# Mixture-of-experts kernel: order of gathers, scatters and row turns around experts 1 to 4

## The chip, the cores and the metric

One core of a Trainium2 chip runs the whole program. The metric is the device time of one execution in microseconds (us). Engine names follow the profile: PE is TensorE, DVE is VectorE, ACT is ScalarE, POOL is GpSimd, SP issues plain DMAs.

## The reference, cut to what matters

```
for e in range(64):                       # first layer, 4096 tokens, top 8 of 64 experts
    inp = xin[e]                          # the 256 rows (tokens) routed to e, 1024 wide
    h   = silu(inp @ wg[e]) * (inp @ wu[e])          # 1024 -> 384, twice
    out = h @ wd[e]                                  # 384 -> 1024
    y[tok] += out * w[tok, e]                        # w: routing weight of the row
x = x + y
# then a second layer: x @ W.T plus adapters, plus a gated low-rank part
```

The rows are first conditioned by a per-sample 128x128 matrix, and a softmax over 64 logits with a top-8 choice decides which rows an expert gets. All of it is float32; the change touches only the expert loop.

## The kernel before, in words

**Stages.** Up to about 173 us the kernel conditions the rows, writes them to the scratch tensor `yd`, and builds the routing tables. Then 64 experts follow, numbered 0 to 63, until about 1789 us. Then comes the second layer.

**One expert on PE.** `up(e)` is three blocks (numbered n = 3e to 3e+2, 128 of the 384 hidden columns each), each with a g half and a u half; `down(e)` follows and takes the hidden rows of one block after another (j = 0, 1, 2). float32 products are made of high and low float32r parts: `HR` and `LR` for weights, the halves of `XX` for the rows, `hH` and `hL` for the hidden values. Two pairs of PSUM banks take the blocks in turn, so block n may start only when `join(n-2)` has emptied its banks. `down(e)` may start on a bank only when `result(e-1)` has read it, and its step j needs `low_h(3e+j)`.

**Weights.** Six units of 768 KB for each expert (`gA uA gB uB dA dB` from expert 2 on). SP loads unit n into one of four `raw` slots once DVE's `split` of unit n-4 is done. `split` on ACT (L1235) writes the high part, `split` on DVE (L1770) the low part.

**Rows.** POOL gathers the rows of expert e in eight indirect DMAs, `gather_x(e, 0)` and `gather_x(e, 1)` with four each (L662), into `Xg`. `turn_x(e, c)` on DVE (L1788) transposes one half into `XR`, `high_x` on ACT (L1263) and `low_x` on DVE (L1794) split it into `XX`. `gather_x(e+1, c)` may be issued only after `turn_x(e, c)`. The row numbers come from `gather_tab(e)` (L637), `count`, `token`, `spread` and `index`.

**Results.** `copy_2(n)` on ACT (L1271) and `join(n)` on DVE (L1806) read the banks of a block; `silu`, `product` (L1812), `high_h`, `low_h` (L1816) make the hidden values. `gather_w(e)` (L672) fetches the routing weights into one of two buffers `Wg`; `column(e)` on DVE (L1837) takes the one column of it that is needed; `result(e, c, h)` on ACT (L1289) scales the output of `down(e)` with it into `ot`, four times for each expert. `scatter(e)` (L684, two DMAs of 512 KB) adds `ot` to the accumulator in HBM. `result(e)` waits for the completion of `scatter(e-1)`, since `ot` is one buffer, and for `column(e)`.

**Order.** Every engine's order is written out by hand. For experts 0 to 2 the lists stand in full; from expert 3 on DVE and ACT run a loop, and POOL's loop starts at `scatter(1)`. Each waits on semaphores, in order: whatever is queued behind a waiting instruction of an engine waits too.

POOL's order before, from the gathers of expert 2 on: x(2), w(1), tab(4), scatter(0), x(3), w(2), w(3), tab(5), scatter(1), x(4), w(4), tab(6), scatter(2), x(5), w(5), and so on.

Of the kernel before, what the change touches and what calls it, by code (L numbers as in the profile page):

```python
# [16 lines left out]
E = 64  # L17
# [42 lines left out]
def adaln_ffn_kernel(nc, x, cond, adap, w0, gate_w, wg, wu, wd, W, A, Bm, scal,  # L60
# [14 lines left out]
    with ExitStack() as ctx:  # L75
# [526 lines left out]
        def _(eng):  # L602
# [63 lines left out]
            def gather_w(e):  # L666
                if e >= 2:
                    eng.wait_ge(s_wc, e - 1)
                else:
                    eng.wait_ge(d_wy, 16 * NB // 4)  # L670
                for c in range(2):
                    eng.indirect_dma_start(Wg[:, e % 2, c, :], None, wdr,  # L672
                                           bass.IndirectOffsetOnAxis(ap=toki[:, c * E + e:c * E + e + 1], axis=0))\
                       .then_inc(d_wg[e % 2], 16)
# [17 lines left out]
            gather_w(0)  # L692
            gather_x(2, 0)
            gather_x(2, 1)
            gather_w(1)
            gather_tab(4)
            scatter(0)
            gather_x(3, 0)
            gather_x(3, 1)
            gather_w(2)  # L700
            gather_w(3)
            for e in range(2, E + 1):
                if e < E - 3:
                    gather_tab(e + 3)
                scatter(e - 1)
                if e + 2 < E:
                    gather_x(e + 2, 0)
                    gather_x(e + 2, 1)
                    gather_w(e + 2)
            eng.wait_ge(d_sc, 32 * E)  # L710

            def gather_a(t):
# [423 lines left out]
        def _(eng):  # L1136
# [223 lines left out]
            for e in range(2, E):  # L1360
                if e < E - 2:
                    spread(e + 2)
                if e == 2:
                    copy_2(6)
                    result(1, 0, 0)
                    silu(6)
                    result(1, 0, 1)
                    result(1, 1, 0)
                    high_h(6)
                    result(1, 1, 1)  # L1370
                    high_x(3, 0)
                    split("dB", 2)
                    high_x(3, 1)
                else:
                    for o in range(4):
                        result(e - 1, o // 2, o % 2)
                    if e < E - 1:
                        high_x(e + 1, 0)
                        high_x(e + 1, 1)
                    if e < E - 1:  # L1380
                        split("dB", e)
                    else:
                        split("dA", e)
                    copy_2(3 * e)
                    if e == E - 1:
                        split("dB", e)
                    silu(3 * e)
                    high_h(3 * e)
                if e + 1 < E:
                    split("gA", e + 1)  # L1390
                copy_2(3 * e + 1)
                silu(3 * e + 1)
                high_h(3 * e + 1)
                if e + 1 < E:
                    split("uA", e + 1)
                else:
                    eng.wait_ge(s_dn, 4 * (E - 1))
                    eng.wait_ge(d_la, 16 * 64)
                    high_w(0)
                copy_2(3 * e + 2)  # L1400
                silu(3 * e + 2)
                high_h(3 * e + 2)
                if e + 1 < E:
                    for k in ("gB", "uB", "dA")[:3 if e + 1 < E - 1 else 2]:
                        split(k, e + 1)
# [167 lines left out]
        def _(eng):  # L1573
# [229 lines left out]
            def join(n):  # L1803
                b0 = 2 * (n % 2)
                eng.wait_ge(s_c2, n + 1)
                eng.tensor_tensor(gu[:, :, :], ps[:, b0:b0 + 2, 0:CAP], gu[:, :, :], ALU.add).then_inc(s_gs, 1)  # L1806
# [71 lines left out]
            product(3)  # L1878
            low_h(3)
            index(3)  # L1880
            split("dB", 1)
            join(4)
            split("gA", 2)
            product(4)
            turn_x(2, 0)
            low_h(4)
            turn_x(2, 1)
            join(5)
            low_x(2, 0)
            product(5)  # L1890
            low_x(2, 1)
            low_h(5)
            column(1)
            for k in ("uA", "gB", "uB"):
                split(k, 2)
            count(4)
            token(4)
            split("dA", 2)
            join(6)
            turn_x(3, 0)  # L1900
            product(6)
            low_h(6)
            turn_x(3, 1)
            index(4)
            low_x(3, 0)
            split("dB", 2)
            join(7)
            count(5)
            product(7)
            token(5)  # L1910
            low_h(7)
            low_x(3, 1)
            column(2)
            column(3)
            split("gA", 3)
            join(8)
            product(8)
# [20 lines left out]
            for e in range(3, E):  # L1938
                if e < E - 1:
                    turn_x(e + 1, 0)  # L1940
                    turn_x(e + 1, 1)
                    if e + 2 < E:
                        index(e + 2)
                    low_x(e + 1, 0)
                    low_x(e + 1, 1)
# [5 lines left out]
                    turn_b(3)  # L1951
                    split("dA", e)
                join(3 * e)
                if e < E - 1:
                    column(e + 1)
                product(3 * e)
                low_h(3 * e)
                split("dB", e)
# [326 lines left out]
```

## Time and profile before

| | |
|---|---|
| median of 3 runs | 2349.42 us (2349.35 to 2352.59) |
| the profiled execution, its own time | 2363.11 us |
| its span, first to last instruction | 2361.4 us |
| busy: PE, DVE, ACT, POOL | 98%, 76%, 60%, 57% |
| PE clock, mean over the span | 0.996 of full speed |

Read it so: the profiled execution is 13.7 us longer than the median run, so differences are taken inside the trace and carried over to the median. PE is busy nearly all the time, so what counts is where PE is idle or at half clock. The timelines give for each instruction its start, its duration and, in brackets, how long its engine had been idle and what ended that.

### The profile page before, as it was taken

Reading aid. Unit: us, or ns where it says so; the run is one execution under the profiler, and the core shown is the slowest. Engines: PE = TensorE matmul, PEld = TensorE weight load, DVE = VectorE, ACT = ScalarE, POOL = GpSimd, SP = SyncE. Lnnn points to the kernel's source line nnn. Section 1 sums busy time; section 2 is a strip of 40 time slices with the busy share of each in tenths; the row PEclk is TensorE's granted clock in tenths of the full one; section 3 lists DMA queues with packets and bytes.
Section 4 is the critical chain, followed back from the end, with each engine's and each line's share of the span. In section 5 each row is a group of like instructions: output and inputs, shape, how many; then the busy total and the mean of one; then the engine's idle time right before and its main releaser. Section 6 shows DMA issues by size and latency. Waiting matters only on the chain.

```text
span 2361.4 us, 35519 instructions
## 1 busy us (share of the span) xinstructions
PE 2319.7 (98%) x12530; PEld 2036.3 (86%) x12530; DVE 1788.6 (76%) x3091; ACT 1419.2 (60%) x2341; POOL 1340.8 (57%) x999
## 2 busy tenths in 40 slices
PE   6989899999999999999999999999999999999999
PEld 4768788888888888888888888888888999999999
DVE  4888788888888888888788888888874268666665
ACT  4766677777777777777777777777763122222221
POOL 4117887777777777877778777777740011111110
PEclk8999999999999999999999999999999999999999
DMA  8999898989999999989989899899895544544452
GB/s 291 379 311 337 260 283 277 283 286 283 279 284 296 271 286 288 278 278 285 284 275 283 283 282 284 272 290 281 274 273 132 112 113 127 146 132 131 132 140 83
DMA packets 256339, 582.35 MB, mean 247 GB/s; under 512 B 85665, under 2 KB 113698, under 8 KB 256162
## 3 DMA queue, kind: packets, MB, share of 16 engines
q1 hardware_dynamic: 189186, 401.19, 52.2%
q0 software_dynamic: 55584, 160.02, 26.3%
q10 hardware_dynamic: 11392, 18.88, 2.1%
q8 instruction: 99, 1.62, 0.3%
q14 instruction: 78, 0.64, 0.1%
HBM read 456.25 MB, written 123.45 MB: 245 GB/s over the span
## 4 chain that ended last, share of the span: by engine, by line
PE 91%; DVE 3%; DMA 2%; issue 2%; ACT 1%; SPq 0%; another core or an unknown queue 0%; ACTq 0%; POOL 0%; DVEq 0%; POOLq 0%
PE ps L891 25%; PE ps L904 21%; PE ps L890 12%; PE ps L1006 9%; PE ps L999 7%; PE ps L951 4%; PE ps L887 4%; PE ps L760 2%; PE ps L989 2%; PE ps L888 2%; PE ps L770 1%; DMA raw<-in_L_ffn_wd 1%; PE ps L963 1%; DVE LR L1770 1%; DMA bx<-in_L_ffn_base_w 1%
## 5 line engine op out<-in xcount | busy, mean ns | idle before, releaser
L891 PE MATMUL ps<-XX,HR 128*128 128x512 f32 x2688 | 959.7, 396 | 0.0
L890 PE MATMUL ps<-XX,LR 128*128 128x256 f32 x2688 | 750.3, 279 | 0.6 <-DVE LR L1770 0.5
L662 POOL DMA_INDIRECT Xg<-yd,idx x504 | 653.4, 1296 | 160.0 <-issue 153.0
L1770 DVE TENSOR_TENSOR LR<-raw,HR 128x1536 fp32r<-128x1536 f32 x384 | 657.5, 1752 | 5.6 <-ACT HR L1235 4.7
L891 PEld LDWEIGHTS ps<-XX,HR 128*128 128x128 f32 x2688 | 505.0, 188 | 104.2
L1235 ACT ACTIVATE HR<-raw 128x1536 fp32r<-128x1536 f32 x384 | 556.9, 1479 | 18.0 <-DMA raw<-in_L_ffn_wd 11.9
L890 PEld LDWEIGHTS ps<-XX,LR 128*128 128x128 f32 x2688 | 507.3, 189 | 18.9 <-DVE LR L1770 1.2
L684 POOL DMA_INDIRECT accd<-ot,toki x128 | 254.0, 1984 | 160.4 <-ACT ot L1289 139.7
L904 PE MATMUL ps<-LR,hH 128*128 128x512 f32 x768 | 302.5, 394 | 0.0
L904 PE MATMUL ps<-HR,hH 128*128 128x512 f32 x768 | 298.6, 389 | 3.0 <-DVE hL L1816 3.0
L904 PE MATMUL ps<-HR,hL 128*128 128x512 f32 x768 | 301.0, 392 | 0.0
L1806 DVE TENSOR_TENSOR gu<-ps,gu 128x512 f32<-128x512 f32 x192 | 132.7, 691 | 161.4 <-ACT gu L1271 146.2
L723 POOL DMA_INDIRECT m8a<-m8d,midx x32 | 36.9, 1153 | 337.3 <-PE ps L963 333.1
L1271 ACT ACTIVATE gu<-ps 128x512 f32<-128x512 f32 x192 | 113.5, 591 | 148.0 <-issue 82.6
L637 POOL DMA_INDIRECT G<-tabd,rowi x124 | 168.8, 1361 | 40.4 <-issue 37.2
L672 POOL DMA_INDIRECT Wg<-wdr,toki x128 | 158.1, 1235 | 39.0 <-issue 38.7
L904 PEld LDWEIGHTS ps<-HR,hH 128*128 128x128 f32 x768 | 144.2, 188 | 33.9 <-DVE hL L1816 4.3
L904 PEld LDWEIGHTS ps<-HR,hL 128*128 128x128 f32 x768 | 144.2, 188 | 33.4
L999 PE MATMUL ps<-MH,xT 128*128 128x392 f32 x640 | 172.7, 341 | 0.0
L1275 ACT ACTIVATE sil<-gu 128x256 f32<-128x256 f32 x192 | 80.2, 418 | 149.6 <-DVE gu L1806 145.6
L904 PEld LDWEIGHTS ps<-LR,hH 128*128 128x128 f32 x768 | 144.4, 188 | 28.8
L887 PE MATMUL ps<-XX,HR 128*128 128x512 f32 x384 | 152.4, 397 | 5.9 <-DVE gu L1806 3.9
(262 smaller groups left out, 3868.8 us busy)
## 6 DMA issues: line engine op xcount, KB each, us to landing
raw<-in_L_ffn_wd SPq DMA_DIRECT2D x128, 768.0 KB
raw<-in_L_ffn_wg SPq DMA_DIRECT2D x126, 768.0 KB
raw<-in_L_ffn_wu SPq DMA_DIRECT2D x126, 768.0 KB
yd<-yrow ACTq DMA_DIRECT2D x32, 512.0 KB
x<-accd SPq DMA_DIRECT2D x32, 512.0 KB, 3.9
out<-x SPq DMA_DIRECT2D x31, 512.0 KB, 5.6
xt<-in_x SPq DMA_DIRECT2D x25, 512.0 KB
accd<-xt SPq DMA_DIRECT2D x25, 512.0 KB
```

The lines of the kernel that those rows point to most:

```text
L637: eng.indirect_dma_start(G[:, e % 2, c, :], None, tab, bass.IndirectOffsetOnAxis(ap=rowi[:, c * E + e:c * E + e + 1], axis=0))\
L662: eng.indirect_dma_start(Xg[:, c, q, :], None, yd4, bass.IndirectOffsetOnAxis(ap=idx4[:, e % 4, i:i + 1], axis=0))\
L672: eng.indirect_dma_start(Wg[:, e % 2, c, :], None, wdr, bass.IndirectOffsetOnAxis(ap=toki[:, c * E + e:c * E + e + 1], axis=0))\
L684: eng.indirect_dma_start(acc, bass.IndirectOffsetOnAxis(ap=toki[:, c * E + e:c * E + e + 1], axis=0), ot[:, c, :], None, compute_op=ALU.ad ...
L887: eng.matmul(bank(out), wh, xx, start=True, stop=False)
L890: eng.matmul(bank(out, 0, CAP), wl, xx[:, 0:CAP], start=False, stop=False)
L891: mm = eng.matmul(bank(out), wh, xx, start=False, stop=(k == 7))
L904: mm = eng.matmul(bank(4 + o), X[:, j, c * P:(c + 1) * P], Wt[:, s, j * 512:(j + 1) * 512], start=(j == 0 and m == 0), stop=(j == 2 and m ...
L999: mm = eng.matmul(bank(BK[region], 0, HG), X[:, k, :], (MH, ML, MH)[m][:, k, a:a + HG], start=(i == 0), stop=(i == 23))
L1006: mm = eng.matmul(bank(BK[region], 0, HG), (XH, XH, XL)[m][:, k, :], (YH, YL, YH)[m][:, k, :], start=(first and i == 0), stop=(i == 11), s ...
L1235: eng.activation(HR[:, (n + 2) % NHL, :], raw[:, n % NRAW, :], ACT.Copy).then_inc(s_H, 1)
L1770: eng.tensor_tensor(LR[:, (n + 2) % NHL, :], raw[:, n % NRAW, :], HR[:, (n + 2) % NHL, :].bitcast(F32), ALU.subtract).then_inc(s_L, 1)
```

## The change

Three things are reordered; no arithmetic is changed.

1. POOL: `gather_tab(4)` and `gather_x(3)` are issued before `scatter(0)`; `gather_tab(5)` and `gather_x(4)` before `scatter(1)`. `gather_w(1)` moves behind `scatter(0)`, `gather_w(2)` and `gather_w(3)` behind `scatter(1)`; from expert 3 on the loop issues `gather_w(e+1)` where it issued `gather_w(e+2)`.
2. DVE: `turn_x(2, 0)`, `turn_x(2, 1)` and `turn_x(3, 0)` go to earlier places, `split("gA", 2)` goes behind `low_h(4)`, `low_x(3, 1)` behind `join(7)`. `column(1)`, `column(2)` and `column(3)` go to later places, and in the loop `column(e)` stands where `column(e+1)` stood.
3. ACT: in iteration 2 the four `result(1)` go from around `copy_2(6)` and `silu(6)` to behind `split("dB", 2)`, and `high_x(3, 1)` goes ahead of that split.

```diff
@@ -692,21 +692,26 @@
             gather_w(0)
             gather_x(2, 0)
             gather_x(2, 1)
-            gather_w(1)
             gather_tab(4)
-            scatter(0)
             gather_x(3, 0)
             gather_x(3, 1)
+            scatter(0)
+            gather_w(1)
+            gather_tab(5)
+            gather_x(4, 0)
+            gather_x(4, 1)
+            scatter(1)
             gather_w(2)
             gather_w(3)
-            for e in range(2, E + 1):
+            for e in range(3, E + 1):
                 if e < E - 3:
                     gather_tab(e + 3)
                 scatter(e - 1)
                 if e + 2 < E:
                     gather_x(e + 2, 0)
                     gather_x(e + 2, 1)
-                    gather_w(e + 2)
+                if e + 1 < E:
+                    gather_w(e + 1)
             eng.wait_ge(d_sc, 32 * E)
 
             def gather_a(t):
@@ -1362,15 +1367,13 @@
                     spread(e + 2)
                 if e == 2:
                     copy_2(6)
-                    result(1, 0, 0)
+                    high_x(3, 0)
                     silu(6)
-                    result(1, 0, 1)
-                    result(1, 1, 0)
                     high_h(6)
-                    result(1, 1, 1)
-                    high_x(3, 0)
+                    high_x(3, 1)
                     split("dB", 2)
-                    high_x(3, 1)
+                    for o in range(4):
+                        result(1, o // 2, o % 2)
                 else:
                     for o in range(4):
                         result(e - 1, o // 2, o % 2)
@@ -1878,40 +1881,39 @@
             product(3)
             low_h(3)
             index(3)
+            turn_x(2, 0)
             split("dB", 1)
             join(4)
+            turn_x(2, 1)
+            product(4)
+            low_h(4)
             split("gA", 2)
-            product(4)
-            turn_x(2, 0)
-            low_h(4)
-            turn_x(2, 1)
             join(5)
             low_x(2, 0)
             product(5)
             low_x(2, 1)
             low_h(5)
-            column(1)
-            for k in ("uA", "gB", "uB"):
-                split(k, 2)
+            split("uA", 2)
+            turn_x(3, 0)
+            split("gB", 2)
+            split("uB", 2)
             count(4)
             token(4)
             split("dA", 2)
             join(6)
-            turn_x(3, 0)
+            turn_x(3, 1)
             product(6)
+            index(4)
             low_h(6)
-            turn_x(3, 1)
-            index(4)
             low_x(3, 0)
+            column(1)
             split("dB", 2)
             join(7)
+            low_x(3, 1)
+            product(7)
             count(5)
-            product(7)
+            low_h(7)
             token(5)
-            low_h(7)
-            low_x(3, 1)
-            column(2)
-            column(3)
             split("gA", 3)
             join(8)
             product(8)
@@ -1938,6 +1940,8 @@
             for e in range(3, E):
                 if e < E - 1:
                     turn_x(e + 1, 0)
+                    if e == 3:
+                        column(2)
                     turn_x(e + 1, 1)
                     if e + 2 < E:
                         index(e + 2)
@@ -1951,8 +1955,7 @@
                     turn_b(3)
                     split("dA", e)
                 join(3 * e)
-                if e < E - 1:
-                    column(e + 1)
+                column(e)
                 product(3 * e)
                 low_h(3 * e)
                 split("dB", e)
```

## Rows read from the trace of the kernel before

**Rows 1.** The page: span, and its part 1 (busy time by engine).
```profile
span 2361.4 us, 35519 instructions
...
PE 2319.7 (98%) x12530; PEld 2036.3 (86%) x12530; DVE 1788.6 (76%) x3091; ACT 1419.2 (60%) x2341; POOL 1340.8 (57%) x999
```

**Rows 2.** By stretch: from:to, length, busy by engine, PEclk, DMA share, GB/s.
```profile
226.41:243.20 16.79, 16.79 (x97) 14.67 (x96) 11.91 (x19) 11.53 (x20) 13.44 (x12) 1.00 0.74 270
243.20:253.89 10.69, 8.42 (x37) 6.61 (x37) 9.57 (x19) 6.30 (x8) 8.86 (x7) 1.00 0.96 231
253.89:276.68 22.79, 18.89 (x99) 16.10 (x98) 15.96 (x24) 14.00 (x23) 18.83 (x14) 0.93 0.94 291
269.26:276.68 7.42, 7.42 (x33) 6.39 (x34) 6.47 (x15) 4.89 (x7) 6.20 (x5) 0.77 1.01 246
...
301.70:1750.00 1448.30, 1448.30 (x7642) 1237.50 (x7641) 1184.87 (x1608) 1060.10 (x1617) 1124.20 (x803) 1.00 0.92 282
```

**Rows 3.** Timeline of PE: start, us, line, operation, [idle before <-releaser].
```profile
251.14 0.50 PE L904 MATMUL ps<-HR,hH 128*128 128x512 f32 x1 [2.27 <-DVE hL L1816]
...
254.01 0.40 PE L887 MATMUL ps<-XX,HR 128*128 128x512 f32 x1
...
269.26 0.51 PE L887 MATMUL ps<-XX,HR 128*128 128x512 f32 x1 [3.90 <-DVE gu L1806]
```

**Rows 4.** Timeline of DVE, experts 1 to 3.
```profile
212.37 1.76 DVE L1770 TENSOR_TENSOR LR<-raw,HR 128x1536 fp32r<-128x1536 f32 x1 [0.81 <-issue]
...
223.41 5.10 DVE L1770 TENSOR_TENSOR LR<-raw,HR 128x1536 fp32r<-128x1536 f32 x3 [0.26 <-ACT HR L1235]
...
238.82 1.25 DVE L1788 STREAM_TRANSPOSE XR<-Xg 128x1024 f32<-128x1024 f32 x1 [2.78 <-DMA Xg<-yd,idx]
...
248.58 0.69 DVE L1806 TENSOR_TENSOR gu<-ps,gu 128x512 f32<-128x512 f32 x1
...
258.64 1.76 DVE L1770 TENSOR_TENSOR LR<-raw,HR 128x1536 fp32r<-128x1536 f32 x1 [2.55 <-ACT HR L1235]
...
264.29 1.25 DVE L1788 STREAM_TRANSPOSE XR<-Xg 128x1024 f32<-128x1024 f32 x1 [2.73 <-DMA Xg<-yd,idx]
```

**Rows 5.** Timeline of ACT, experts 2 and 3.
```profile
240.10 1.07 ACT L1263 ACTIVATE XX<-XR 128x1024 fp32r<-128x1024 f32 x1 [1.61 <-issue]
...
242.45 0.57 ACT L1271 ACTIVATE gu<-ps 128x512 f32<-128x512 f32 x1
...
257.12 1.49 ACT L1235 ACTIVATE HR<-raw 128x1536 fp32r<-128x1536 f32 x1 [3.72 <-DMA raw<-in_L_ffn_wd]
...
260.11 2.42 ACT L1289 ACTIVATE ot<-ps,wcol 128x512 f32<-128x512 f32 x4
...
265.57 1.06 ACT L1263 ACTIVATE XX<-XR 128x1024 fp32r<-128x1024 f32 x1 [2.09 <-issue]
...
267.90 0.58 ACT L1271 ACTIVATE gu<-ps 128x512 f32<-128x512 f32 x1
```

**Rows 6.** Timeline of POOL: gathers and scatters issued.
```profile
212.55 2.40 POOL L637 DMA_INDIRECT G<-tabd,rowi  x1 [0.30 <-issue]
...
232.62 0.95 POOL L662 DMA_INDIRECT Xg<-yd,idx  x1 [0.30 <-issue]
...
244.76 1.58 POOL L684 DMA_INDIRECT accd<-ot,toki  x1 [0.30 <-issue]
...
258.48 0.95 POOL L662 DMA_INDIRECT Xg<-yd,idx  x1 [0.30 <-issue]
```

**Rows 7.** Timeline of SP's queue: weight loads issued.
```profile
248.70 4.46 SPq L435 DMA_DIRECT2D raw<-in_L_ffn_wd  x2
```

**Rows 8.** DMA traffic by stretch (last two columns), as in rows 2.
```profile
241.00:242.00 1.00, 1.00 (x8) 0.86 (x7) 1.00 (x2) 1.00 (x2) 1.00 (x1) 1.00 0.00 0
...
248.00:252.00 4.00, 1.73 (x8) 1.11 (x7) 3.04 (x5) 2.20 (x4) 3.33 (x3) 1.00 1.04 202
...
253.00:260.00 7.00, 7.00 (x41) 6.02 (x40) 4.45 (x3) 3.12 (x9) 5.47 (x6) 1.00 1.05 396
```

## The prediction

> **What bounds the kernel now.** I read the page first, then the busy time by stretch, then PE's timeline, and then went back through DVE, ACT, POOL and the DMA traffic to what was late. PE is busy 98% of the span [rows 1]. By stretch, it has no idle time at all from 301.70 to 1750 us [rows 2], so nothing that is moved in the loop can gain there; it can only lose. Around the change the picture is different. One expert takes PE 25.02 us: 16.79 for its three blocks [rows 2] and 8.23 for its down part (25.02 less 16.79). From the start of up(2) at 226.41 to the start of down(3) at 276.68 there are two ups and one down, 41.8 us of work, in 50.27 us [rows 2]: 8.5 us are lost. They lie in three places:
> - 2.27 us before step j = 2 of down(2), which waits for low_h(8) [rows 3] and makes the 8.23 into 10.69 [rows 2];
> - 3.90 us before block n = 11, the last of up(3), which waits for join(9) [rows 3];
> - 1.83 us in that block, which takes 7.42 us in place of a third of 16.79, at a mean granted clock of 0.77: after the idle 3.90 us the clock stood at its lower level, 1.2 GHz, for a time [rows 2].
>
> The rest, about 0.5 us, is small gaps. Both waits go back to rows that arrive late. DVE waited 2.78 us for the second half of expert 3's rows and 2.73 us for that of expert 4 [rows 4]; ACT's high_x stood idle behind them for 1.61 and 2.09 us [rows 5]. A third thing is late before block 11: ACT waited 3.72 us for the weight unit dA(3) [rows 5], and DVE 2.55 us behind it [rows 4]. So 8.5 us, 0.36% of the run, is the most that the change can remove.
>
> **Rows gathered earlier.** How long a gather takes to issue follows from DVE: the issue at 212.55 began inside the split of 212.37 to 214.13 [rows 4] and ended at 214.95 [rows 6], 0.8 after it, where one outside a split takes 0.95 and a gap of 0.30 [rows 6]. From 212.55 to 244.76 POOL issued 19 DMAs one behind another [rows 6], 1.7 us each on average, gaps included. After the change gather_x(3, 0) can start when turn_x(2, 0), now at 211.6, is through, at 212.9. Eight issues at 1.7 end at 226.3. In the trace a last gather landed 5.25 us after its issue ended (233.57 to 238.82) and another 4.86 us after (259.43 to 264.29) [rows 4, 6]; so expert 3's rows are there by 231.5 at the latest, and turn_x(3, 1), due after join(6) at 233.9, does not wait. That removes the 2.78. turn_x(4, 1) loses its 2.73 in the same way: its gathers end near 249.3 in place of 259.43.
>
> **What takes the place of it in iteration 2.** turn_x(3, 0), 1.25 us [rows 4], now stands between the splits of uA(2) and gB(2). The three splits took 5.10 from 223.41, 1.70 each [rows 4], so gB(2) ends at 223.4 + 1.7 + 1.2 + 1.7 = 228.0 or 228.1. PE wants it half way through its first g half, a quarter of a 5.6 us block: 226.41 + 1.4 = 227.8. That is a new stall of 0.3 to 0.4 us; I take 0.4. The bounds are 0 (the split 0.3 earlier) and 1.0 (turn_x(3, 0) waits for its rows). The same insertion delays token(4) and spread(4), which follow the splits: these end at 228.5 + 1.2 = 229.7, count(4), token(4) and spread(4) take some 2.9 more, and copy_2(6) starts at about 232.6. From there ACT has, in order, 0.5 + 1.0 + 0.4 (copy, high_x, silu), 1.0 of waiting for product(6), 0.4 + 1.0 + 1.4 (high_h, high_x, split dB), 2.4 for the four results and 1.4 for split gA(3), the durations by [rows 5]: 9.5 us, and copy_2(7) starts at 242.1. Before it started at 242.45 [rows 5]. **This is the point of the forecast: the wait is gone, but the four results, 2.4 us, now stand in the gap.** Before, low_h(8) was ready for PE 8.7 us after copy_2(7) began (251.14 less 242.45) [rows 3, 5], and DVE has the same instructions in between (its join(8) comes at 248.58 behind split gA(3) [rows 4]; they are only reordered). So PE goes on at 250.9 where it is ready at 249.1 (0.4 later than before). The stall is 1.8 in place of 2.27, down(2) gains nearly nothing, and up(3) starts at 253.8 in place of 254.01 [rows 3]. Bounds: 1.3 to 2.3.
>
> **The scatters, and what waits for them.** scatter(0) is issued from 226.3 to 231.4. scatter(1) was issued by 246.34 [rows 6], and the traffic stood at 202 GB/s from 248 to 252 and at 396 from 253 on [rows 8]: I read the low rate as the accumulating scatter, and so its end as 5.5 to 6 us after its last issue. scatter(0) is then complete at 237 to 238, just before ACT reaches result(1), which needs it, at 238.2. Behind scatter(0) POOL has w(1), tab(5) and x(4): 12 issues at 1.5 to 1.7, so scatter(1) is issued from about 249.6 to 254.1 (its second DMA falls into split uA(3)) and complete at 260.0. result(2) waits for it. gather_w(2) comes after, its issue ends at 257 to 258.5, and column(2) and then result(2) wait for that too. Without these waits DVE would have split dA(3) done at 257.4 and turn_x(4, 0) at 258.6, and result(2) could start at 258.8. With them I take 260.6, the lower bound for the start being 258.8 and the upper 262. Before it was 260.11 [rows 5].
>
> The Trainium skill (DMA: Bandwidth & Descriptors, Queues, rings and completion order) says that a semaphore increment lands only after every earlier write of the same DMA engine. By it the routing weights behind a scatter are not usable until the scatter has been written, so column(2) could not start before about 260 either; by the row alone it could be 2 us earlier. No row here shows it. The sum would be the same by both, since result(2) waits for the scatter itself; a forecast that counts on early weights alone would be 1.8 us too low.
>
> **Weight unit dA(3).** SP issued it at 248.70 [rows 7], when split gA(3) was through; ACT took it at 257.12 [rows 5], 8.4 later, with the DMA engines full [rows 8]. Now it is issued at 248.5, and gather_x(4), 1 MB, is out of its way (the DMA engines moved nothing at 241 to 242 before [rows 8]; the gathers now fill that time), while scatter(1) is still in it. I take 254 to 257 for its landing. Up to 254.1 it costs nothing; at 257 it gives a start of result(2) at 261.4, within the bounds above.
>
> **Block 11.** From the start of result(2) to PE's restart it was 9.15 us (260.11 to 269.26) [rows 3, 5], of which 2.09 was the wait for expert 4's rows [rows 5], now gone: 7.06 is left. PE restarts at 267.7. It is ready at 253.8 + 11.35 = 265.1 (11.35 is 254.01 to 265.36, the restart less 3.90 [rows 3]). The stall is 2.5 us in place of 3.90. Does the clock fall? After 3.90 idle it did; after 2.27 idle, at 251.14, it stood at full speed (a block of normal length follows) [rows 2, 3]. 2.5 is nearer to 2.27: I take full speed, and keep the other for the range, 1.83. down(3) starts at 267.7 + 5.6 = 273.3 in place of 276.68, a gain of 3.4.
>
> **The rest.** Expert 4 has then 3.4 us less before it; DVE waits in it for gathers that now end some 3 us sooner, so I cost it at nothing. In the loop gather_w(e+1) is issued some 10 us before column(e+1); the cover is a full iteration of POOL, and the cost stays nothing up to that. column(63) moves into the last iteration: 0.2 us on DVE, off PE's chain.
>
> **Sum** in the profiled execution (2361.4 span, 2363.11 in all): 0.4 lost at gB(2), 0.4 to 0.6 gained at low_h(8), 1.4 at block 11, 1.8 from the clock, in all 3.4: 2359.7. Carried to the median of the runs, 2349.42 - 3.4 = **2346.0**.
>
> **Rivals.**
> - *Forecast, 50%.* Both stalls shrink in part. With result(2) anywhere from 258.8 to 262 and the clock either way the gain is 1.3 to 5.0: 2344.4 to 2348.1.
> - *The waits go altogether, 22%.* The scatters complete early, dA(3) lands before 254 and ACT gets through iteration 2 sooner. For it speaks that the gathers really were the last to arrive in both waits [rows 4]; against it, that result(1) and result(2) are in ACT's order ahead of the copies. Gain 5.0 to 8.0 (8.5 less 0.4 to 0.5): 2341.4 to 2344.4.
> - *The waits change their name and not their length, 20%.* result(2) starts at 262 or later because scatter(1), the weights behind it or dA(3) come late; PE idles 3.9 again and the clock falls. 2348.4 to 2350.4.
> - *Slower, 8%.* gather_w(1) and scatter(0) share the DMA engines with three weight units issued from 228 to 233 (2.3 MB, 11 us at 202 GB/s [rows 8]). If column(1) or scatter(0) is ready only at 244 in place of 238.2, results, copy_2(7) and low_h(8) move by 5.8 one for one: a stall of 7.6 and a fall of the clock, 12.3 lost in place of 8.5, 2353.2. It decides from 241.5 on. By the skill's rule above this is the likelier way for it.
>
> The chances follow: under 0.2% (4.7 us, about what a measurement of this kernel can tell) lies between the forecast and the second case, so faster is 22% and a little of the forecast, 26%; slower by as much is most of the last case, 6%; within 0.2% is 68%. The range leaves out the fastest part of the second case and the last: 2342.0 to 2350.6.
>
> **What would show it.** No DVE wait for Xg before 270; expert 3's gathers issued from 213 to 226; a PE gap of 0.3 to 0.5 near 228 on LR; PE waiting for hL near 249 for 1.3 to 2.3; result(2) near 260.6 behind column(2) or a DMA; PE's wait for join(9) near 2.5 and no half clock; no idle PE after expert 4. The forecast is wrong if a wait on Wg or on a scatter lasts over 2 us, if the clock falls, or if PE idles anywhere in the loop.

## The result, and the profile after

The changed kernel takes 2359.04 us (median of 11 runs, 2354.82 to 2364.73), the kernel before 2352.39 us (11 runs, 2347.56 to 2355.78). The ratio is 1.0031, with a 95% interval of 1.0023 to 1.0039: slower by some 7 us, more than the 0.2% bound. The forecast, 2346.0 and most likely within 0.2%, was wrong. It went the way of the last rival, which had been given 8%.

The page of the changed kernel, beside [rows 1]:

```profile
span 2363.0 us, 35519 instructions
PE 2322.5 (98%) x12530; PEld 2039.0 (86%) x12530; DVE 1788.2 (76%) x3091; ACT 1418.4 (60%) x2341; POOL 1340.0 (57%) x999
```

Here up(0) starts at 167.02, where it started at 172.84 before, so 5.82 is to be added to a time below to compare it with the rows of before. By stretch, as in [rows 2]: up(2) with the wait behind it; down(2); up(3); block 11, the end of up(3); the loop; then a part of down(2), near half clock (0.55).

```profile
220.36:240.60 20.24, 17.20 (x98) 14.51 (x96) 12.14 (x19) 9.17 (x18) 16.59 (x12) 1.00 0.88 257
240.60:254.02 13.42, 10.52 (x36) 7.85 (x37) 9.67 (x17) 8.94 (x12) 10.98 (x9) 0.87 0.80 188
254.02:273.72 19.70, 17.09 (x98) 14.64 (x97) 14.11 (x24) 12.75 (x23) 12.43 (x9) 1.00 0.94 279
268.02:273.72 5.70, 5.70 (x33) 4.98 (x34) 4.70 (x14) 3.74 (x7) 4.59 (x4) 1.00 0.93 198
301.70:1750.00 1448.30, 1448.30 (x7645) 1237.70 (x7644) 1185.47 (x1607) 1060.56 (x1614) 1123.63 (x804) 1.00 0.92 282
246.40:249.40 3.00, 3.00 (x8) 2.37 (x9) 2.77 (x5) 1.44 (x3) 2.39 (x3) 0.55 0.82 104
```

The loop has no idle PE, as before. From the first matmul of up(2) to that of down(3) it is 53.36 us in place of 50.10 (the stretches of [rows 2] end 0.17 us later and give 50.27). In this execution up(3) improved, 19.70 in place of 22.50, and block 11 ran at full clock (5.70 in place of 7.42). All of that and more was lost ahead of it: 3.45 us more than 16.79 in up(2), where there was no loss, and 13.42 in place of 10.81 in down(2). The timelines of PE, DVE and ACT, beside [rows 3 to 5]:

```profile
222.38 0.38 PE L895 MATMUL ps<-XX,LR 128*128 128x256 f32 x1 [0.47 <-DVE LR L1773]
240.60 0.51 PE L909 MATMUL ps<-HR,hH 128*128 128x512 f32 x1 [2.57 <-DVE LR L1773]
246.40 0.54 PE L909 MATMUL ps<-HR,hH 128*128 128x512 f32 x1 [2.77 <-DVE hL L1819]
268.02 0.50 PE L892 MATMUL ps<-XX,HR 128*128 128x512 f32 x1 [2.61 <-DVE gu L1809]
```
```profile
228.18 1.24 DVE L1791 STREAM_TRANSPOSE XR<-Xg 128x1024 f32<-128x1024 f32 x1
...
238.71 0.17 DVE L1840 COPY wcol<-Wg 128x2 f32<-128x2 f32 x1 [6.95 <-DMA Wg<-wdr,toki]
238.79 1.75 DVE L1773 TENSOR_TENSOR LR<-raw,HR 128x1536 fp32r<-128x1536 f32 x1
```
```profile
238.97 2.42 ACT L1294 ACTIVATE ot<-ps,wcol 128x512 f32<-128x512 f32 x4 [6.47 <-issue]
241.26 1.50 ACT L1240 ACTIVATE HR<-raw 128x1536 fp32r<-128x1536 f32 x1
242.64 0.61 ACT L1276 ACTIVATE gu<-ps 128x512 f32<-128x512 f32 x1
...
256.49 1.49 ACT L1240 ACTIVATE HR<-raw 128x1536 fp32r<-128x1536 f32 x1 [3.10 <-DMA raw<-in_L_ffn_wd]
...
261.06 2.42 ACT L1294 ACTIVATE ot<-ps,wcol 128x512 f32<-128x512 f32 x4 [1.61 <-issue]
```

ACT is ready for result(1) at 232.50, which is 238.3 in the time of before and was forecast as 238.2. So the two engines' own order is not what is late. DVE reaches column(1) at 231.76 and stands 6.95 us until the routing weights are there. Two things are queued behind it. On DVE it is the low part of split dB(2), at 238.79, which PE needs to begin down(2): that is the 2.57. On ACT it is result(1), and behind result(1) copy_2(7), at 242.64, and through it join(7), copy_2(8) and low_h(8): that is the 2.77. ACT's 6.47 are labelled "issue", but result(1) starts 0.1 us after column(1) ends. The rows came in time: turn_x(3, 1) at 228.18 has no wait in brackets.

POOL's timeline, beside [rows 6], and three pieces of the chain of work that ended last (start, length, what):

```profile
220.66 3.17 POOL L684 DMA_INDIRECT accd<-ot,toki  x1 [0.30 <-issue]
224.13 1.57 POOL L684 DMA_INDIRECT accd<-ot,toki  x1 [0.30 <-issue]
226.00 1.84 POOL L672 DMA_INDIRECT Wg<-wdr,toki  x1 [0.30 <-issue]
228.15 0.98 POOL L672 DMA_INDIRECT Wg<-wdr,toki  x1 [0.31 <-issue]
```
```profile
224.13 13.83 DMA accd<-ot,toki
237.96 1.00 issue
...
248.70 7.77 DMA raw<-in_L_ffn_wd
```

scatter(0) was issued as forecast (53.6 to 58.7 us after the start of up(0); forecast 53.5 to 58.6). But it was written only at 237.96, 12.3 us after the issue of its second DMA ended at 225.70; the forecast had 5.5 to 6. DVE went on with the weights issued behind it at 238.7, 9.6 after their own issue had ended.

### The profile page after: what moved, and what is told of

Read it like the earlier page. It is cut to its first block, busy times and chain, and to the rows that moved or that the text cites. A ratio compares the mean times of both kernels' runs of the same rounds, so it can differ in the third digit from the quotient of the medians.

```text
span 2363.0 us, 35519 instructions
## 1 busy us (share of the span) xinstructions
PE 2322.5 (98%) x12530; PEld 2039.0 (86%) x12530; DVE 1788.2 (76%) x3091; ACT 1418.4 (60%) x2341; POOL 1340.0 (57%) x999
## 4 chain that ended last, share of the span: by engine, by line
PE 90%; DMA 3%; DVE 2%; issue 2%; ACT 1%; POOL 1%; ACTq 0%; SPq 0%; DVEq 0%; POOLq 0%
PE ps L896 25%; PE ps L909 21%; PE ps L895 12%; PE ps L1011 9%; PE ps L1004 7%; PE ps L956 4%; PE ps L892 4%; PE ps L765 2%; PE ps L994 2%; PE ps L893 2%; POOL Xg L662 1%; PE ps L775 1%; PE ps L968 1%; DMA bx<-in_L_ffn_base_w 1%; DMA accd<-ot,toki 1%
## 5 line engine op out<-in xcount | busy, mean ns | idle before, releaser
L896 PE MATMUL ps<-XX,HR 128*128 128x512 f32 x2688 | 958.4, 396 | 0.0
L1280 ACT ACTIVATE sil<-gu 128x256 f32<-128x256 f32 x192 | 80.2, 418 | 151.6 <-DVE gu L1809 151.5
L1294 ACT ACTIVATE ot<-ps,wcol 128x512 f32<-128x512 f32 x256 | 155.2, 689 | 9.5 <-issue 8.1
```

Source lines behind the costliest of these rows:

```text
L896: mm = eng.matmul(bank(out), wh, xx, start=False, stop=(k == 7))
L1294: eng.activation(ot[:, c, h * 512:(h + 1) * 512], bank(4 + 2 * c + h), ACT.Copy, scale=wcol[:, c * E + e:c * E + e + 1]).then_inc(s_out, 1)
```

## The experiments

The table gives when each stage starts, in us from the start of up(0), in one profiled execution of each kernel; up(0) itself comes at 160 to 174 us. Without any wait, up(e) takes 16.79 [rows 2] and an expert 25.02 (up(4) to up(5) in most lines), so down(e) takes 8.23. The ratios are medians of several runs against the kernel before on the same chip.

| kernel | up(2) | down(2) | up(3) | down(3) | up(4) | up(5) | ratio, interval |
|---|---|---|---|---|---|---|---|
| before | 53.6 | 70.4 | 81.2 | 103.7 | 111.9 | 136.9 | |
| before_again | 52.1 | 70.0 | 82.4 | 102.7 | 110.9 | 135.9 | |
| loop_only | 53.4 | 70.4 | 82.9 | 100.5 | 108.8 | 133.8 | 1.0002, 0.9993 to 1.0011 |
| after | 53.3 | 73.6 | 87.0 | 106.7 | 114.9 | 140.0 | 1.0031, 1.0023 to 1.0039 |
| after_again | 53.0 | 73.0 | 86.4 | 108.6 | 116.8 | 141.9 | |
| after_3 | 53.5 | 73.0 | 86.6 | 110.6 | 118.9 | 143.9 | 1.0030, 1.0019 to 1.0041 |
| head_only | 53.4 | 72.8 | 86.2 | 107.4 | 115.6 | 140.7 | 1.0026, 1.0014 to 1.0037 |
| w1_ahead | 54.1 | 72.1 | 86.3 | 107.6 | 115.9 | 140.9 | 1.0024, 1.0012 to 1.0035 |
| two_ot | 54.1 | 71.6 | 81.2 | 110.4 | 118.6 | 143.6 | 1.0035, 1.0023 to 1.0047 |
| between | 53.3 | 70.4 | 82.9 | 107.5 | 115.7 | 140.7 | 1.0029, 1.0020 to 1.0038 |
| x3_alone | 52.3 | 77.3 | 90.8 | 107.5 | 115.8 | 140.8 | 1.0016, 1.0007 to 1.0025 |
| w12_ahead | 53.3 | 72.6 | 87.6 | 105.5 | 113.7 | 138.8 | 1.0028, 1.0018 to 1.0038 |
| w12_two_ot | 53.2 | 70.2 | 83.0 | 100.8 | 110.0 | 137.4 | 1.0023, 1.0012 to 1.0035 |
| between_w | 52.8 | 75.8 | 88.8 | 107.4 | 115.7 | 140.7 | 1.0028, 1.0018 to 1.0037 |
| rows_first | 52.9 | 69.7 | 86.1 | 102.9 | 111.1 | 143.1 | 1.0031, 1.0019 to 1.0043 |
| no_sc01 | 52.3 | 69.4 | 79.0 | 96.6 | 104.9 | 129.9 | 0.9988, 0.9978 to 0.9997 |
| no_sc0 | 53.5 | 70.6 | 80.2 | 105.5 | 113.7 | 138.7 | 1.0025, 1.0016 to 1.0034 |
| col1_late | 53.2 | 71.7 | 85.9 | 107.1 | 115.4 | 140.4 | 1.0022, 1.0013 to 1.0032 |

**Head or loop.** head_only is the changed kernel with the loop of before from expert 6 on; loop_only is the kernel before with the changed loop.

```diff
 head_only, against the changed kernel
-                if e + 1 < E:
+                if e <= 4:
                     gather_w(e + 1)
+                if 4 <= e and e + 2 < E:
+                    gather_w(e + 2)
...
 loop_only, against the kernel before
-                    gather_w(e + 2)
+                if e == 2:
+                    gather_w(4)
+                if e >= 4 and e + 1 < E:
+                    gather_w(e + 1)
```

> The kernel before once more, for a second profile. From the start of up(0) to that of up(5) the first profile took 136.94 us, the changed kernel 139.97; from join(186) to the end before took 618.4 us, the changed one 622.8. If the 4.4 us at the end belong to the change, this profile repeats 618.4 within 0.5. If they are the scatter of the DMA traffic from one execution to the next, it may lie anywhere from 617 to 624. The start of up(0) was at 172.84 and 167.02 us, and differs again by some us.

> The order of the changed kernel up to expert 5, the loop of the kernel before from expert 6 on (routing weights two experts ahead, none gathered in iteration 62). Theory A, the routing weights queued behind scatter(0) cost the first experts 3 us and the end is independent of the loop: 3 us over before, or with the end's scatter the same as the changed kernel, ratio 1.0013 to 1.0031, and column(1) waits 6 to 7 us. Theory B, the loop's later gather costs 4.4 us at the end: this kernel is 3 us over before, ratio 1.0013, and its end takes 618.4 us.

> The order of the kernel before up to expert 3, and from then on routing weights gathered one expert ahead, as in the changed kernel. Theory A: the same as before, ratio 1.000 within 0.001, up(0) to up(5) 136.9 us. Theory B: 4.4 us slower, ratio 1.0019, with the join(190) wait of PE near 4 us at the end.

The loop is innocent: loop_only stands at 1.0002, and from up(5) to down(63) 17 of the 18 executions, of whatever kernel, take 1467.9 to 1468.1 us (w12_ahead 1468.6). head_only has the loss, 1.0026. In it the profile names the scatter for ACT's wait before result(1), although column(1), late for its weights, ended only 0.1 us before:

```profile
233.35 2.42 ACT L1296 ACTIVATE ot<-ps,wcol 128x512 f32<-128x512 f32 x4 [6.09 <-DMA accd<-ot,toki]
```

**Which of the two is late, the weights or the scatter.** w1_ahead issues gather_w(1) ahead of scatter(0); two_ot does so too and gives results 1 and 3 a buffer of their own, so that result(1) need not wait for scatter(0), nor result(2) for scatter(1).

```diff
 w1_ahead, against the changed kernel
+            gather_w(1)
             scatter(0)
-            gather_w(1)
...
 two_ot, against w1_ahead
-                    eng.wait_ge(d_sc, 32 * e)
+                    eng.wait_ge(d_sc, 32 * e if e > 4 else 32 * (e - 1))
...
+        def obuf(e, c):
+            if e in (1, 3):
+                return (bmR if c else laR)[:, :, :, :].rearrange("p q a r -> p (q a r)")
+            return ot[:, c, :]
```

> The changed kernel with the two gathers of expert 1's routing weights issued just ahead of scatter(0) in place of just behind it. Theory A (they were late because they stood behind the scatter): column(1) no longer waits 6.95 us, low_h(8) and split dB(2) come some 5 us earlier, no PE wait on LR at the start of down(2), up(0) to up(5) about 134 to 135 us, 5 to 6 us under the changed kernel, ratio to before 0.998 to 1.001. Rival: result(1) waits for scatter(0) itself, which is issued just as late; then the results start near 238 again, only split dB(2) is free, and up(0) to up(5) stays at 137 to 140.

> The changed kernel with gather_w(1) ahead of scatter(0), and with a second buffer for the results of experts 1 and 3, so that result(1) no longer waits for scatter(0), nor result(2) for scatter(1). Theory C (the loss is result(1) waiting until scatter(0) has landed, 4.99 us on ACT in the run before this): no wait before result(1), PE idles at most 2 us in down(2) and 2.5 us before block 11, the clock does not fall, up(0) to up(5) 133 to 135 us against 140.9, ratio to before 0.998 to 1.000. Rival: another wait of the new order, the splits or the weight units, holds PE as long; then it stays at 138 or more.

In w1_ahead column(1) waits for nothing, and nothing is gained: up(5) comes at 140.9, not at the 134 to 135 that was expected. result(1) now waits for the scatter itself:

```profile
231.53 2.42 ACT L1294 ACTIVATE ot<-ps,wcol 128x512 f32<-128x512 f32 x4 [4.99 <-DMA accd<-ot,toki]
```

So both are late, and the scatter alone suffices for the loss. two_ot removes both waits, and up(3) starts at 81.2. But the kernel was expected at 133 to 135 for up(5) and has 143.6, for now the weights of expert 2, behind scatter(1), come late, with no wait for a scatter beside them; PE stands 9.43 us before block 11. Late weights alone suffice as well:

```profile
267.54 0.17 DVE L1845 COPY wcol<-Wg 128x2 f32<-128x2 f32 x1 [8.65 <-DMA Wg<-wdr,toki]
```

**Scatters in other places.** x3_alone is the kernel before with x(3) ahead of scatter(0) and nothing else; between lets each scatter pass between the two halves of the rows; between_w does so with the weights of experts 1 and 2 ahead of the scatters; w12_ahead and w12_two_ot put w(2) ahead of scatter(0) in w1_ahead and two_ot; rows_first is the kernel before with the second buffer, and rows and weights ahead of each scatter.

```diff
 x3_alone, against the kernel before
-            scatter(0)
             gather_x(3, 0)
             gather_x(3, 1)
+            scatter(0)
...
 between, against the changed kernel
             gather_x(3, 0)
+            scatter(0)
             gather_x(3, 1)
-            scatter(0)
             gather_w(1)
             gather_tab(5)
             gather_x(4, 0)
+            scatter(1)
             gather_x(4, 1)
-            scatter(1)
...
 w12_ahead, against w1_ahead; w12_two_ot, against two_ot
             gather_w(1)
+            gather_w(2)
             scatter(0)
...
             scatter(1)
-            gather_w(2)
             gather_w(3)
...
 between_w, against the changed kernel
             gather_x(3, 0)
-            gather_x(3, 1)
+            gather_w(1)
             scatter(0)
-            gather_w(1)
+            gather_x(3, 1)
             gather_tab(5)
+            gather_w(2)
             gather_x(4, 0)
+            scatter(1)
             gather_x(4, 1)
-            scatter(1)
-            gather_w(2)
             gather_w(3)
...
 rows_first, against the kernel before (with obuf as in two_ot)
-            scatter(0)
             gather_x(3, 0)
             gather_x(3, 1)
             gather_w(2)
             gather_w(3)
+            scatter(0)
+            gather_tab(5)
+            gather_x(4, 0)
+            gather_x(4, 1)
+            gather_w(4)
+            scatter(1)
-            for e in range(2, E + 1):
+            for e in range(3, E + 1):
```

> The changed kernel with each scatter between the two halves of the next gathers: x(3,0), scatter(0), x(3,1), w(1), tab(5), x(4,0), scatter(1), x(4,1), w(2), w(3). scatter(0) is issued some 7 us sooner. Theory C: it has landed when ACT comes to result(1), if it takes 9 us from its last issue; no wait there or under 1 us, expert 3's second half is still in time (landing near 61 us after up(0), wanted at 61), up(0) to up(5) 133 to 136 us, ratio 0.998 to 1.001. Rival: result(1) is not what matters, 139 or more.

> The kernel before with one move: gather_x(3) ahead of scatter(0). Rows of expert 3 no longer late on DVE. Theory C: result(1), which still stands right behind copy_2(6) on ACT, now waits for a scatter issued some 12 us later and blocks ACT for 8 to 12 us; up(0) to up(5) 143 to 148 us, ratio 1.003 to 1.005. Rival (a scatter lands within 6 us, only the changed places of the other steps cost): 136 to 139 us.

> The changed kernel with the routing weights of experts 1 and 2 gathered ahead of scatter(0). One buffer for the results, as in the changed kernel. Theory D (what is issued behind a scatter lands only after it, and result(1) and result(2) wait for the scatter itself): result(1) waits about 5 us for scatter(0) as in the run with only expert 1's weights ahead, column(1) and column(2) do not wait, up(0) to up(5) 139 to 142 us, ratio 1.001 to 1.003. Rival (only the weights were late): 134 to 136 us.

> As the run before, with the second result buffer for experts 1 and 3. Theory D: both waits are gone, result(1) near 65 and result(2) near 89 to 91 us after up(0), PE idle under 2 us in down(2) and under 2.5 before block 11, no fall of the clock, up(0) to up(5) 132 to 135 us, ratio 0.998 to 1.000. Rival: a further wait takes their place as column(2) did with the second buffer alone; 138 or more.

> The changed kernel with x(3,0), w(1), scatter(0), x(3,1), tab(5), w(2), x(4,0), scatter(1), x(4,1), w(3); one result buffer. Theory D: column(1) and column(2) do not wait, scatter(1) is the last thing that result(2) waits for, up(0) to up(5) 134 to 138 us, ratio 0.999 to 1.001; but the second halves of the rows now stand behind a scatter and land 9 us or more after it, so turn_x(3,1) waits 1 to 3 us.

> The kernel before in its DVE and ACT order, with x(3), w(2) and w(3) ahead of scatter(0), tab(5), x(4) and w(4) ahead of scatter(1), and the second result buffer for experts 1 and 3, so that results wait for no late scatter. Theory D: it has what the change was after without its waits; no DVE wait for Xg up to expert 4, up(0) to up(5) 131 to 134 us against 134 to 137 of before, ratio 0.997 to 0.999. Rival: ACT's and DVE's own order bounds experts 2 and 3 whatever arrives when; 135 to 137 us, ratio 1.000.

None of the six beats the kernel before. between, between_w, rows_first and w12_two_ot reach up(5) later than was expected, x3_alone earlier, w12_ahead 0.2 us earlier. In x3_alone result(1) stands at its old place, and ACT waits 11.45 us there. In w12_ahead, with both weights ahead, result(1) and result(2) still wait for their scatters, 6.77 and 2.75. First x3_alone, then w12_ahead:

```profile
243.72 0.69 ACT L1289 ACTIVATE ot<-ps,wcol 128x512 f32<-128x512 f32 x1 [11.45 <-DMA accd<-ot,toki]
```
```profile
233.45 2.42 ACT L1294 ACTIVATE ot<-ps,wcol 128x512 f32<-128x512 f32 x4 [6.77 <-DMA accd<-ot,toki]
...
254.49 2.42 ACT L1294 ACTIVATE ot<-ps,wcol 128x512 f32<-128x512 f32 x4 [2.75 <-DMA accd<-ot,toki]
```

In the others what stands behind a scatter on POOL's queue is the next to be late. One line each of between, between_w, w12_two_ot and rows_first, all of DVE:

```profile
264.39 0.17 DVE L1840 COPY wcol<-Wg 128x2 f32<-128x2 f32 x1 [3.51 <-DMA Wg<-wdr,toki]
```
```profile
232.75 1.25 DVE L1791 STREAM_TRANSPOSE XR<-Xg 128x1024 f32<-128x1024 f32 x1 [9.41 <-DMA Xg<-yd,idx]
```
```profile
279.76 1.25 DVE L1796 STREAM_TRANSPOSE XR<-Xg 128x1024 f32<-128x1024 f32 x1 [2.84 <-DMA Xg<-yd,idx]
```
```profile
239.10 0.35 DVE L1832 TENSOR_SCALAR_CACHE_REDUCE Gj<-G,slot 128x128 f32<-128x128 f32 x1 [6.97 <-DMA G<-tabd,rowi]
```

By up(5) w12_two_ot comes nearest, with 137.4; it loses 2.4 in expert 4, where the rows of expert 5 stand behind a late scatter(2). By the ratio it is x3_alone, with 1.0016, though it has up(5) at 140.8: one execution and the median of several differ by some us. These are waits that were seen; that each came from the scatter and not from the other traffic of its time is shown only by the next group, and there for scatter(0) and scatter(1).

**No scatter in the way.** no_sc01 leaves out the first two scatters of the changed kernel, no_sc0 the first; POOL still waits for their results, and every later wait for a count of scatters is lowered to match.

```diff
                     eng.wait_ge(s_out, 4 * e + 2 * c + 2)
+                    if e < 2:          # no_sc0: e < 1
+                        continue
                     eng.indirect_dma_start(acc,
...
-                if e:
-                    eng.wait_ge(d_sc, 32 * e)
+                if e > 2:              # no_sc0: e > 1, and e - 1 below
+                    eng.wait_ge(d_sc, 32 * (e - 2))
```

> The changed kernel with the first two scatters left out (the output lacks experts 0 and 1); nothing else is moved, and POOL still waits for their results before it goes on. Theory E (all of the loss comes from what waits for the two early scatters to be written): column(1) and the four results do not wait, the earlier rows keep their gain, and the forecast's own course appears: up(3) starts 81 us after up(0) (80 to 82), up(4) 107 to 109, up(5) 132 to 134 (before: 135.9 and 136.9), and the ratio is 0.9985 to 1.0005. Theory F (the new order on DVE and ACT costs by itself, scatters or not): up(3) not before 84, up(5) 137 or later, ratio 1.002 or more. If the head is short and the ratio is still over 1.001, the rest of the loss is outside experts 0 to 4.

> The changed kernel with scatter(0) alone left out (the output lacks expert 0). Theory E: column(1) and result(1) do not wait, so up(3) starts at 80 to 82; scatter(1) and the weights of experts 2 and 3 behind it are as before this edit, so block 11 still waits some 2 to 4 us, and up(5) is at 134 to 137. Theory F: up(3) not before 84. Rival within E: if the delay sits in scatter(1) as much as in scatter(0), up(5) is at 138 or later.

no_sc01 settles that the loss hangs on the two scatters, and not on the new order of DVE and ACT. column(1) and column(2) do not wait, no wait of PE over 1.2 us is left in experts 1 to 4, the clock stays up, and the ratio is 0.9988, though with less work than the kernel before. From up(2) to up(4), against 58.35 in before and 61.60 in after (50.04 without any wait):

```profile
218.16:270.74 52.58, 50.89 (x265) 42.69 (x264) 42.74 (x65) 36.89 (x59) 40.97 (x31) 1.00 0.83 256
```

The up(5) it reaches, 129.9, lies below the 132 to 134 that was expected. It is 5.7 less than the mean of 136.9, 135.9 and 133.8 in the kernel before and loop_only, of which the medians show only 1.9; what took the rest is not shown.

Leaving a scatter out takes away the wait for it, its traffic and also its issue on POOL. The issue is the lesser part: in no_sc0 that of the weights of expert 1 ended 58.8 us after up(0), 3.3 sooner than in after, and column(1) ran at 64.4, 7.3 sooner. The wait and the traffic are not told apart by these runs.

In no_sc0 experts 1 and 2 have no wait over 1.2 us (up(3) at 80.2), and the loss comes one scatter later, as its rival had it, with up(5) at 138.7: scatter(1) takes 11.7 us from the start of its second DMA, and column(2) follows 1 us behind.

```profile
240.82 11.69 DMA accd<-ot,toki
```
```profile
253.53 0.17 DVE L1842 COPY wcol<-Wg 128x2 f32<-128x2 f32 x1 [5.45 <-DMA Wg<-wdr,toki]
```

**The queue on DVE.** col1_late has column(1) behind split dB(2).

```diff
-            column(1)
             split("dB", 2)
+            column(1)
             join(7)
```

> The changed kernel with column(1) behind split dB(2) on DVE in place of ahead of it, nothing else. The split that down(2) needs is then not queued behind the wait for the routing weights. Theory G (the queue on DVE only moves the loss; the end is set by ACT's result(1), which needs column(1) in any case): down(2) starts 71 us after up(0) in place of 73.6, PE then waits once, 4.8 to 6 us, for low_h(8), and up(3) starts at 86.3 to 88 as before this edit; up(5) 139 to 141.5; ratio 1.0022 to 1.0035. Rival (the 2.57 us are a loss of their own): up(3) at 84 to 85.5, ratio 1.0022 or less.

> The changed kernel once more, with five rounds, for the size. Between the starts of up(0) and up(5) it should take 139.5 to 142 us (three profiled executions of the kernel before and its like: 133.8 to 136.9), so 3 to 6 us of the 6.7 to 7.4 by which the medians differ. Theory H (the rest, some 2 to 3 us, is the wait of the router's transposes for the last join, seen at 4.2 and 3.9 us in two executions of the changed kernel): it shows again over 3 us here, the tail from down(63) on is 587 us or more. Rival (the tail differs by chance between executions): the wait is under 2.5 us and the tail 583.5 to 586.5. Ratio 1.002 to 1.004 by both.

> The changed kernel a second time, for its profile: if column(1) behind scatter(0) is what costs, its wait is again 5 to 8 us and up(0) to up(5) is 139 to 141 us; the stretch from down(63) to the end, 588.1 us the first time against 583.7 in the first profile of before, falls anywhere in 583 to 588 if it only scatters.

Down(2) starts at 71.7 in place of 73.0 to 73.6, with 1.30 us of idle PE, now for result(1); then PE waits 3.61 for low_h(8), where 4.8 to 6 was expected (2.77 in the first execution of the changed kernel), and up(3) starts at 85.9 in place of 86.4 to 87.0. up(3) lies halfway between the two theories, up(5) in the range of the first. So, as far as one execution tells, the split behind column(1) moved the loss more than it made it: 0.5 to 1.1 us are its own. The two idle times on PE:

```profile
233.24 0.47 PE L909 MATMUL ps<-HR,hH 128*128 128x512 f32 x1 [1.30 <-ACT ot L1294]
239.84 0.51 PE L909 MATMUL ps<-HR,hH 128*128 128x512 f32 x1 [3.61 <-DVE hL L1819]
```

**The size.** The three executions of the changed kernel reach up(5) at 140.0, 141.9 and 143.9, mean 141.9; the last two lie above what was expected for them. The two of the kernel before and loop_only, whose order is the same up to expert 3, are at 136.9, 135.9 and 133.8, mean 135.5. The difference, 6.4 us, is nearly the 6.7 to 8.1 between the medians; with head_only, which has the changed order here and 140.7, it is 6.0. One execution of each would have shown 3.0. What comes from the last down on differs as well (583.7 to 588.6 us over all kernels; 583.7 and 586.9 in the two of the kernel before). In two executions of the changed kernel the router's transposes waited 4.2 and 3.9 us for the last join, which looked like a second cost; in after_3 they waited 2.4, for another transfer, and before_again has 3.1 without the change. It is not shown to belong to the change. The rest of the spread lies ahead of up(0), at 160 to 174 us, where nothing was changed; on the chip of two_ot, between, x3_alone and after_again it is 172 to 174, which is most of why their medians are longer.

## Why the prediction was wrong, step by step

- **The rows: right.** The gathers of expert 3 ran from 206.8 to 220.4 here, turn_x(3, 1) did not wait, nor did turn_x(4, 0) and turn_x(4, 1). The new stall at gB(2) is 0.47, forecast 0.4. scatter(0)'s issue was met within 0.2.
- **"Its end as 5.5 to 6 us after its last issue": this step failed.** It was read from a drop and rise of the traffic [rows 8], with no wait in the trace that ended on a scatter. Measured from the end of the second issue it was 12.3 us for scatter(0) in after, 9.6 in after_3 and 8.9 in after_again. The rate of [rows 8] is that of all queues together, so 396 GB/s from 253 on does not say that the scatter was through. In after scatter(0) was ready at 237.96, or 243.8 in the time of before, past the 241.5 from which the last rival decides. That rival's time, 2353.2, is 3.8 above the median it started from; the measured difference is about 7.
- **The last rival's reason** was that the scatter shares the DMA engines with three weight units. What the runs show fits it: in the eight executions whose chain of work goes over scatter(0), the issue of its second DMA ended between 58.7 and 65.7 us after up(0), but it was complete between 69.4 and 71.8 in all of them. On the whole, the later it was issued, the less time it took, down to 6.0 us in w12_ahead. But no run moved the weight units away from it, so why scatter(0) was not done before 69 stays open.
- **The weights behind the scatter.** They came at 238.7, 0.7 after the scatter; in no_sc0 the weights of expert 2 came 1.0 after scatter(1); in no_sc01, with no scatter ahead, column(1) had nothing to wait for 5.6 us after the end of their issue. The Trainium skill (DMA: Bandwidth & Descriptors, Queues, rings and completion order) says that the increment lands only after every earlier write of that DMA engine. These runs agree with it, though none tests it apart from the traffic. The prediction used the rule for experts 2 and 3 and named it for its last rival, but left the sum for expert 1 to the traffic.
- **The queue behind column(1) on DVE: overlooked.** The prediction followed the results on ACT, and not split dB(2), which now stood behind column(1) and which down(2) needs. It brought a wait of 2.57 us before down(2), where none was forecast; col1_late shows that without it most of the time is lost a little later all the same.
- **copy_2(7) at 242.1: wrong by the same step.** It began at 242.64, which is 248.5 in the time of before. "The stall is 1.8" became 2.57, 2.77 and some 2.4 at half clock (13.42 less 8.23 less 2.77). With the scatters gone, down(2) took 9.6, 1.4 more than 8.23, so for the order itself the forecast of 1.8, with bounds of 1.3 to 2.3, was a little high.
- **result(2) at 260.6, block 11 at 2.5 and no fall of the clock: met once, by luck.** result(2) came 94.0 us after up(0), where the forecast, on an up(3) 6 us earlier, had 87.8. It did not wait for scatter(1) and the weights, as the sum had it: column(2) had no wait, and the chain of work goes from dA(3), which landed 7.8 us after its issue (the forecast's range is 5.5 to 8.5), through its split and turn_x(4, 0) to result(2). The stall was 2.61, and block 11 kept its clock. But with the same order the stall was 3.58 in after_again, 4.32 in after_3 and 2.54 in head_only, and in all three the clock fell behind it. That is part of why the loss is 6.4 us and not the 3.0 of the first execution.
- **The most that could be gained, 8.5 us:** right within 0.2 for that execution. From up(2) to up(4) it lost 8.3 (58.35 less 50.04), before_again 8.8 and loop_only 5.3 (55.34 less 50.04), so a single trace does not give this size.

The form of the forecast was sound, since one of its rivals named the mechanism and the point from which it decides; the 8% hung on a completion time that had never been measured.

## What to carry to other kernels

When transfers are reordered around an accumulating scatter, first find a wait in a trace that ended on the scatter's completion; if there is none, measure it by moving one consumer up, because the traffic's rate does not show it. Measure it at the place where the scatter will stand, for here the time from issue to completion ran from 6 to 12 us with what else was under way. Count everything issued behind the scatter on the same queue as arriving no sooner than it, small gathers too, and give the first consumer of each its place by that. A blocked instruction is to be followed on every engine that waits for it and through what is queued behind it there.

## What the runs showed of the hardware that was not expected

- An accumulating scatter of two DMAs of 512 KB, with weight loads and gathers beside it, was complete 8.05 to 13.83 us after the start of its second DMA. For scatter(0) it was 13.83, 12.17 and 11.48 in after, after_3 and after_again, 12.03 in head_only, 11.97 in col1_late, 11.68 in w1_ahead, 8.96 in x3_alone and 8.05 in w12_ahead; for scatter(1) it was 11.88 in two_ot, 11.69 in no_sc0 and 9.56 in w12_ahead.
- The length of one idle time of PE does not tell whether the clock falls. At block 11, with the same order of work, it stayed up in after behind 2.61 us of idle PE and fell in head_only behind 2.54 (0.73 on average over the next 2.85 us). In loop_only it stood at half speed for a time after 2.30 us. The first row is of loop_only behind its 2.30, the second of after behind its 2.61 (the third number from the end is the granted clock):

```profile
238.97:243.42 4.45, 4.45 (x13) 3.49 (x14) 4.45 (x3) 2.24 (x2) 3.54 (x4) 0.62 1.03 358
```
```profile
268.02:270.87 2.85, 2.85 (x16) 2.53 (x17) 1.96 (x4) 2.36 (x4) 2.24 (x3) 1.00 1.05 190
```

- The prediction took full speed at block 11 because 2.5 was near to 2.27. The outcome of the first execution agreed; the reason did not hold. What decides between the two levels (1.2 and 2.4 GHz) stays open here.
